# Row maxima of the attention scores: one pair of 64-row matmuls and one reduction of two PSUM banks, in place of two 128-row matmuls and two reductions

## The chip, the cores and the metric

The kernel runs on one core of one Trainium2 chip. The metric is the device time of a run in microseconds, lower is better. The kernel before took 4128.93 us, the median of three runs (4126.80 to 4134.72).

## The reference

```
x: (16, 32, 32, 512) float32, 16 batches of 1024 tokens with 512 channels
qkv = x @ w_qkv + b_qkv                       # 8 heads, q, k, v of 64 channels each
attn = softmax(q @ k.T * 64 ** -0.5)          # 1024 x 1024 for each head
res = (attn @ v) @ w_out + b_out + x
```

All inputs and the output are float32. For every batch and head the softmax runs over 1024 keys for each of 1024 queries.

## The kernel before, in words

Every value that goes through TensorE in the projections and scores is split into a high part (f32r) and a low part, so that a product is several matmuls. Vectors q and k of a head lie in 64 partitions. `k_lo_hi` holds the low part of k in partitions 0 to 63 and the high part in 64 to 127; `q_hi_hi` holds the high part of q twice, in 0 to 63 and again in 64 to 127 (the second copy is made by a DMA, L355). Both are double buffered by head.

A batch is 8 heads of 2 halves of the queries; head and half together are a **unit**, 16 in a batch. A unit has 512 queries (4 tiles of 128) and goes over 1024 keys in 4 **steps** of 256 keys, 64 steps in a batch. The work is laid out by hand in **slots**, one for each step, with some ahead of the first step (slots -5 to -1) and some behind the last. Each engine walks through the same slots, and within one engine everything runs in the written order. In slot s TensorE does, in this order (L605 on):

- the "early" row-maximum tiles of a unit that starts later (L543),
- parts of the q and k projection of a coming head, 12 matmuls for each half of the tokens (L514; in slots with s mod 8 = 0 after the scores),
- the scores of step s + 1 (L572, L574: two key tiles, each two matmuls of 128 rows and 512 columns, each into one of three score banks),
- the "late" row-maximum tiles,
- in one slot of four, a transpose of the unit's row maxima (L552),
- the product of the probabilities and v for step s - 1 (L595, L598: 16 short f16 matmuls).

ScalarE computes the exponentials twice for each score bank (L696 in f32, L697 in f16). GpSimd (L411) or VectorE (L826) takes their difference, the low part of the probabilities, for which L598 waits.

The row maximum is the shift of the softmax. Before the scores of a unit start, it is taken from separate scores: for each of the 4 query tiles and each half of the keys one matmul (L545) with 128 rows in the contraction, `q_hi_hi` against `k_lo_hi`, so q_hi k_lo + q_hi k_hi. This makes 8 tiles for a unit, tile n being query tile n // 2 and key half n % 2. They use PSUM banks 4 and 5 in turn. VectorE reduces each tile of 128 x 512 to one column (L804), and after the eighth joins the pairs (L810). The transpose (L552) turns the 4 columns of maxima into 4 rows, and VectorE writes them, negated, into rows of `q_shift` (L817), by which the second matmul of each score (L574) subtracts the maximum.

A bank is claimed by `claim_max` (L475): tile number n in the order of all maxima and shifts of the batch waits until VectorE has finished number n - 2. So one tile can be written while the one before it is reduced. The order is in `MAX_TILES` (L60): for unit u the slots 4u - 5 to 4u - 2 hold the tiles (0, 1) early and 2 late; (3, 4) early; (5, 6) early and 7 late; none. The transpose of unit u stands in slot 4u - 2. Units 0 and 1 have orders of their own (L61).

## Time and profile before

| what | value |
|---|---|
| median of three runs | 4128.93 us |
| span of the profiled execution | 4126.3 us |
| TensorE busy | 95% |
| ScalarE busy | 75% |
| VectorE busy | 65% |
| GpSimd busy | 52% |
| mean granted TensorE clock | 0.997 |

The profile shows one execution. The busy time of an engine is the time in which at least one of its instructions was under way. Matmuls overlap, and their ends are modelled, so what one costs is read as the distance from its start to the start of the next one. A wait is listed as idle time ahead of an instruction, with the instruction that released it.

### The profile page before, as it was taken

Reading aid. Unit: us, or ns where it says so; the run is one execution under the profiler, and the core shown is the slowest. Engines: PE = TensorE matmul, PEld = TensorE weight load, DVE = VectorE, ACT = ScalarE, POOL = GpSimd, SP = SyncE. Lnnn points to the kernel's source line nnn. Section 1 sums busy time; section 2 is a strip of 40 time slices with the busy share of each in tenths; the row PEclk is TensorE's granted clock in tenths of the full one; section 3 lists DMA queues with packets and bytes.
Section 4 is the critical chain, followed back from the end, with each engine's and each line's share of the span. In section 5 each row is a group of like instructions: output and inputs, shape, how many; then the busy total and the mean of one; then the engine's idle time right before and its main releaser. Section 6 shows DMA issues by size and latency. Waiting matters only on the chain.

```text
span 4126.3 us, 94307 instructions
## 1 busy us (share of the span) xinstructions
PE 3939.8 (95%) x29964; PEld 3064.1 (74%) x29964; DVE 2694.0 (65%) x4395; ACT 3076.7 (75%) x5269; POOL 2135.8 (52%) x1144
## 2 busy tenths in 40 slices
PE   6999999999999999999999999999999999999999
PEld 5777777777777777777777777777777777777777
DVE  5757757576575765757657576675766757667576
ACT  4967949689495895958859588595886959769597
POOL 1645626456263563636636366363663626536265
PEclk9999999999999999999999999999999999999999
DMA  3011020110202102020021201212011121120201
GB/s 97 22 53 43 18 77 23 58 37 17 78 22 66 29 19 75 22 73 22 24 70 23 72 22 29 65 24 73 22 37 58 24 71 24 37 58 22 63 22 42
DMA packets 100814, 179.08 MB, mean 43 GB/s; under 512 B 16192, under 2 KB 16192, under 8 KB 100288
## 3 DMA queue, kind: packets, MB, share of 16 engines
q1 hardware_dynamic: 100288, 172.29, 14.7%
q8 instruction: 302, 4.95, 0.5%
q14 instruction: 224, 1.84, 0.1%
HBM read 71.57 MB, written 33.55 MB: 25 GB/s over the span
## 4 chain that ended last, share of the span: by engine, by line
PE 74%; issue 8%; ACT 8%; DVE 4%; POOL 4%; ACTq 0%; DMA 0%; DVEq 0%; SPq 0%; POOLq 0%
PE psum L514 33%; PE psum L545 10%; PE psum L572 8%; PE psum L595 8%; PE psum L574 7%; ACT p_hi L697 4%; PE psum L598 4%; POOL p_lo L411 4%; ACT p_full L696 3%; PE psum L528 2%; DVE max_parts L804 1%; DVE q_shift L783 1%; ACT k_lo_hi L667 1%; DVE xT_lo L767 1%; DVE q_shift L817 1%
## 5 line engine op out<-in xcount | busy, mean ns | idle before, releaser
L411 POOL TENSOR_TENSOR p_lo<-p_full,p_hi 128x1024 f16<-128x1024 f32 x752 | 1610.5, 2144 | 1452.7 <-ACT p_hi L697 1452.7
L804 DVE TENSOR_REDUCE max_parts<-psum 128x1 f32<-128x512 f32 x2048 | 1341.4, 686 | 534.0 <-PE psum L545 522.6
L696 ACT ACTIVATE p_full<-psum,prob_bias 128x512 f32<-128x512 f32 x2048 | 1434.9, 701 | 123.2 <-PE psum L574 90.6
L697 ACT ACTIVATE p_hi<-psum,prob_bias 128x512 f16<-128x512 f32 x2048 | 1435.6, 701 | 0.0
L595 PEld LDWEIGHTS psum<-v_parts,p_hi 128*128 128x128 f16 x8192 | 714.8, 97 | 284.4 <-issue 133.2
L595 PE MATMUL psum<-v_parts,p_hi 128*128 128x129 f16 x8192 | 854.4, 221 | 35.3 <-POOL p_lo L411 20.3
L572 PE MATMUL psum<-q_hi_hi,k_lo_hi 128*128 128x512 f32 x2048 | 846.2, 413 | 43.6 <-ACT p_hi L697 38.9
L598 PE MATMUL psum<-v_parts,p_lo 128*128 128x65 f16 x8192 | 819.8, 192 | 0.0
L574 PE MATMUL psum<-q_shift,k_shift 128*128 128x512 f32 x2048 | 804.7, 393 | 0.0
L545 PE MATMUL psum<-k_lo_hi,q_hi_hi 128*128 128x512 f32 x2048 | 757.1, 429 | 19.7 <-DVE q_shift L817 11.9
L598 PEld LDWEIGHTS psum<-v_parts,p_lo 128*128 128x128 f16 x8192 | 723.6, 98 | 2.4
L418 POOL TENSOR_TENSOR o_heads<-o_sum,inv_sum 128x256 f32<-128x256 f32 x256 | 364.6, 1424 | 371.7 <-DVE o_sum L835 371.7
L572 PEld LDWEIGHTS psum<-q_hi_hi,k_lo_hi 128*128 128x128 f32 x2048 | 384.3, 188 | 206.6 <-ACT p_hi L697 145.8
L545 PEld LDWEIGHTS psum<-k_lo_hi,q_hi_hi 128*128 128x128 f32 x2048 | 361.7, 188 | 99.7 <-DVE q_shift L817 23.5
L574 PEld LDWEIGHTS psum<-q_shift,k_shift 128*128 128x128 f32 x2048 | 385.5, 188 | 62.6
L514 PE MATMUL psum<-xT_hi,wqkv_hi 128*128 128x512 f32 x1024 | 413.0, 403 | 0.0
L514 PE MATMUL psum<-xT_hi,wqkv_lo 128*128 128x512 f32 x1024 | 409.3, 400 | 0.0
L514 PE MATMUL psum<-xT_lo,wqkv_hi 128*128 128x512 f32 x1024 | 402.7, 393 | 0.0
L655 ACT CAST xT_hi<-psum 128x512 fp32r<-128x512 f32 x256 | 141.9, 601 | 327.3 <-PE psum L528 326.9
L826 DVE TENSOR_TENSOR p_lo<-p_full,p_hi 128x1024 f16<-128x1024 f32 x272 | 331.4, 1218 | 38.1 <-ACT p_hi L697 38.1
L672 ACT CAST v_parts<-psum 128x512 f16<-128x512 f32 x128 | 75.2, 587 | 358.6 <-PE psum L514 358.6
L817 DVE TENSOR_TENSOR q_shift<-psum,minus_block 4x512 fp32r<-4x512 f32 x256 | 173.6, 678 | 156.8 <-PE psum L552 153.6
(61 smaller groups left out, 4308.2 us busy)
## 6 DMA issues: line engine op xcount, KB each, us to landing
x_in<-in_x SPq DMA_DIRECT2D x128, 256.0 KB, 4.0
k_shift<-k_lo_hi SPq DMA_DIRECT2D x256, 128.0 KB, 2.2
q_hi_hi<-q_hi_hi SPq DMA_DIRECT2D x256, 128.0 KB, 2.3
y_tile<-in_x SPq DMA_DIRECT2D x128, 256.0 KB, 2.7
result<-y_tile SPq DMA_DIRECT2D x128, 256.0 KB, 2.3
o_heads<-in_L_conv_w_qkv SPq DMA_DIRECT2D x12, 256.0 KB, 4.1
o_heads<-in_L_conv_w_out SPq DMA_DIRECT2D x4, 256.0 KB, 4.3
out_bias<-in_L_conv_b_out SPq DMA_DIRECT2D x1, 256.0 KB, 6.2
```

The source lines that it names most:

```text
L411: nc.gpsimd.tensor_tensor(p_lo[:, s % P_SLOTS, :, :], p_full[:, s % 2, :, :], p_hi[:, s % P_SLOTS, :, :], ALU.subtract).then_inc(p_lo_read ...
L418: nc.gpsimd.tensor_tensor(o_heads[:, half * Q_TILES:(half + 1) * Q_TILES, h * DIM:(h + 1) * DIM], o_sum[:, :, :], inv_sum[:, :].rearrange( ...
L514: matmul = nc.tensor.matmul(fill_bank(w), a, b, start=n == 0, stop=n == TERMS - 1)
L545: nc.tensor.matmul(dst, q_hi_hi[:, h % 2, q0:q0 + P], k_lo_hi[:, h % 2, k_half * HALF:(k_half + 1) * HALF], start=True, stop=True).then_in ...
L572: nc.tensor.matmul(score_bank(tile), k_lo_hi[:, h % 2, keys], q_hi_hi[:, h % 2, cols], start=True, stop=False)
L574: nc.tensor.matmul(score_bank(tile), k_shift[:, h % 2, keys], q_shift[:, h % 2, cols], start=False, stop=True).then_inc(scores_ready, 1)
L595: nc.tensor.matmul(pv[:, bank, col:col + PV_W], p_hi[:, s % P_SLOTS, n, qs], v_parts[:, kt, h, 0:PV_W], start=kt == 0 and qt % 2 == 0, sto ...
L598: last = nc.tensor.matmul(pv[:, bank, col + DIM:col + PV_W], p_lo[:, s % P_SLOTS, n, qs], v_parts[:, kt, h, DIM:PV_W], start=False, stop=k ...
L696: nc.scalar.activation(p_full[:, s % 2, n, :], score_bank(tile), ACT.Exp, scale=SCALE, bias=prob_bias[:, :])
L697: nc.scalar.activation(p_hi[:, s % P_SLOTS, n, :], score_bank(tile), ACT.Exp, scale=SCALE, bias=prob_bias[:, :]).then_inc(exp_done, 1)
L804: nc.vector.reduce_max(max_parts[:, u % 2, q_tile, k_half:k_half + 1], max_bank(w), AX.X).then_inc(max_tile_done, 1)
L826: nc.vector.tensor_tensor(p_lo[:, s % P_SLOTS, :, :], p_full[:, s % 2, :, :], p_hi[:, s % P_SLOTS, :, :], ALU.subtract).then_inc(p_lo_read ...
```

## The change

The 8 tiles of a unit become 4, one for each query tile. A tile is now two matmuls with 64 rows each. The first has partitions 0 to 63: q_hi against `k_upper`, a new copy of the high part of k for keys 0 to 511, written to bank 4. The second has partitions 64 to 127: the second copy of q_hi against the high part of k for keys 512 to 1023 as it lies in `k_lo_hi`, written to bank 5. The term q_hi k_lo is no longer in the maximum. Only the second matmul signals. VectorE reduces both banks at once, 128 x 1024 to one column of `row_max`; the partial maxima, the joining reduction (L810) and its semaphore are gone. The tiles of a unit stand in these slots: 0 early and 1 late; 2 early; 3 early; none (units 0 and 1: one early tile in each slot). `claim_max` now waits until VectorE has finished number n - 1, since both banks belong to each tile. The copy `k_upper` is made by one more DMA for each head, between the two DMAs of the first half of the tokens, and the maxima wait for it. The diff, without its blank lines:

```diff
@@ -57,9 +37,11 @@
-MAX_TILES = (((0, 1), (2,)), ((3, 4), ()), ((5, 6), (7,)), ((), ()))
-MAX_TILES_OF_UNIT = {0: (((0, 1), ()), ((2, 3), ()), ((4, 5), ()), ((6, 7), ())),
-                     1: (((0, 1), ()), ((2, 3), ()), ((4, 5), (6,)), ((7,), ()))}
+MAX_TILES = (((0,), (1,)), ((2,), ()), ((3,), ()), ((), ()))
+MAX_TILES_OF_UNIT = {0: (((0,), ()), ((1,), ()), ((2,), ()), ((3,), ())),
+                     1: (((0,), ()), ((1,), ()), ((2,), ()), ((3,), ()))}
 def max_tiles_of_slot(s, late=False):
@@ -68,7 +50,7 @@
     if not 0 <= unit < UNITS:
         return []
     tiles = MAX_TILES_OF_UNIT.get(unit, MAX_TILES)
-    return [("row_max", unit, n // 2, n % 2) for n in tiles[slot][late]]
+    return [("row_max", unit, n) for n in tiles[slot][late]]
 def shift_unit_of_slot(s):
@@ -212,8 +194,6 @@
 def attention_block(nc: bass.Bass, x, w_qkv, b_qkv, w_out, b_out, out):
     f32, f32r, f16 = mybir.dt.float32, mybir.dt.float32r, mybir.dt.float16
     ALU, ACT, AX = mybir.AluOpType, mybir.ActivationFunctionType, mybir.AxisListType
-    assert MAXES % 2 == 0
     x_tok = x.rearrange("b h w c -> b (h w) c")
     out_tok = out.rearrange("b h w c -> b (h w) c")
@@ -235,6 +215,7 @@
         o_heads = sb("o_heads", [P, TOKEN_TILES, CH], f32)
         v_parts = sb("v_parts", [P, TOKEN_TILES, HEADS, V_WIDTH], f16)
         k_lo_hi = sb("k_lo_hi", [P, 2, TOKENS], f32r)
+        k_upper = sb("k_upper", [DIM, 2, HALF], f32r)
         k_shift = sb("k_shift", [P, 2, TOKENS], f32r)
         q_hi_hi = sb("q_hi_hi", [P, 2, TOKENS], f32r)
         q_shift = sb("q_shift", [P, 2, TOKENS], f32r)
@@ -247,7 +228,6 @@
         v_bias = sb("v_bias", [P, CH_TILES], f32)
         out_bias = sb("out_bias", [P, CH], f32)
         minus_block = sb("minus_block", [Q_TILES, Q_TILES, P], f32)
-        max_parts = sb("max_parts", [P, 2, Q_TILES, 2], f32)
         row_max = sb("row_max", [P, 2, Q_TILES], f32)
         o_lo = sb("o_lo", [P, Q_TILES, DIM], f32)
         o_sum = sb("o_sum", [P, Q_TILES, DIM], f32)
@@ -263,8 +243,7 @@
         psum = ctx.enter_context(nc.psum_tensor("psum", [P, 8, HALF], f32))
         pv = psum[:, 6:8, :]
-        def max_bank(w):
-            return psum[:, 4 + MAX_AT[w] % 2, :]
+        max_banks = psum[:, 4:6, :]
         def fill_bank(w):
             return psum[:, FILL_BANK[w], :]
@@ -294,6 +273,7 @@
         hi_done = sem("hi_done")
         max_tile_ready = sem("max_tile_ready")
         max_tile_done = sem("max_tile_done")
+        k_upper_ready = sem("k_upper_ready")
         k_shift_ready = [sem(f"k_shift_ready{k}") for k in range(HALVES)]
         q_hi_hi_ready = [sem(f"q_hi_hi_ready{k}") for k in range(HALVES)]
         scores_ready = sem("scores_ready")
@@ -301,7 +281,6 @@
         p_lo_ready = [sem(f"p_lo_ready{k}") for k in range(2)]
         DVE, POOL = False, True
         pv_done = sem("pv_done")
-        max_ready = sem("max_ready")
         o_lo_ready = sem("o_lo_ready")
         o_free = sem("o_free")
         o_ready = sem("o_ready")
@@ -352,6 +331,9 @@
                         sp.wait_ge(hi_done, signals(i, HIS, HI_AT["qk", h, half] + 1))
                         sp.dma_start(k_shift[DIM:P, h % 2, cols].bitcast(f32),
                                      k_lo_hi[DIM:P, h % 2, cols].bitcast(f32)).then_inc(k_shift_ready[half], 16)
+                        if half == 0:
+                            sp.dma_start(k_upper[:, h % 2, :].bitcast(f32),
+                                         k_lo_hi[DIM:P, h % 2, cols].bitcast(f32)).then_inc(k_upper_ready, 16)
                         sp.dma_start(q_hi_hi[DIM:P, h % 2, cols].bitcast(f32),
                                      q_hi_hi[0:DIM, h % 2, cols].bitcast(f32)).then_inc(q_hi_hi_ready[half], 16)
@@ -475,12 +457,11 @@
                 def claim_max(w):
                     n = MAX_AT[w]
-                    if n < 2:
+                    if n == 0:
                         pe.wait_ge(fill_done, signals_led(i, FILLS, 0))
                     else:
-                        pe.wait_ge(max_tile_done, signals_led(i, MAXES, n - 1))
-                    return max_bank(w)
+                        pe.wait_ge(max_tile_done, signals_led(i, MAXES, n))
                 def three_terms(a_hi, a_lo, b_hi, b_lo):
@@ -535,21 +516,23 @@
                         projection(w, first, last)
                 def row_max_tile(w):
-                    _, u, q_tile, k_half = w
+                    _, u, q_tile = w
                     h, half = divmod(u, HALVES)
-                    dst = claim_max(w)
+                    claim_max(w)
                     pe.wait_ge(fill_done, signals_led(i, FILLS, FILL_AT["qk", h, 1] + 1))
                     pe.wait_ge(q_hi_hi_ready[half], signals(i, HEADS * 16, (h + 1) * 16))
+                    pe.wait_ge(k_upper_ready, signals(i, HEADS * 16, (h + 1) * 16))
                     q0 = half * HALF + q_tile * P
-                    nc.tensor.matmul(dst, q_hi_hi[:, h % 2, q0:q0 + P],
-                                     k_lo_hi[:, h % 2, k_half * HALF:(k_half + 1) * HALF],
+                    nc.tensor.matmul(max_banks[:, 0, :], q_hi_hi[0:DIM, h % 2, q0:q0 + P],
+                                     k_upper[:, h % 2, :], start=True, stop=True)
+                    nc.tensor.matmul(max_banks[:, 1, :], q_hi_hi[DIM:P, h % 2, q0:q0 + P],
+                                     k_lo_hi[DIM:P, h % 2, HALF:2 * HALF],
                                      start=True, stop=True).then_inc(max_tile_ready, 1)
                 def shift_tile(u):
-                    dst = claim_max(("shift", u))
-                    pe.wait_ge(max_ready, signals_led(i, UNITS, u + 1))
-                    nc.tensor.transpose(dst[0:Q_TILES, 0:P], row_max[:, u % 2, :],
+                    claim_max(("shift", u))
+                    nc.tensor.transpose(max_banks[0:Q_TILES, 0, 0:P], row_max[:, u % 2, :],
                                         identity[:, :]).then_inc(max_tile_ready, 1)
                 def step_scores(s):
@@ -757,7 +740,7 @@
             dve.wait_ge(bias_product, 1)
             nc.vector.tensor_tensor(out_bias[:, :], psum[:, 5, :], out_bias[:, :], ALU.add).then_inc(bias_ready, 1)
             dve.wait_ge(consts_ready, 4)
-            for led in (fill_done, max_tile_done, p_lo_ready[DVE], o_free, max_ready):
+            for led in (fill_done, max_tile_done, p_lo_ready[DVE], o_free):
                 dve.sem_inc(led)
             with dve.Fori(0, BATCH) as i:
                 def transposed_lo(w):
@@ -795,20 +778,11 @@
                     {"x_transpose": transposed_lo, "o_transpose": transposed_lo, "v": v_lo, "qk": qk_lo,
                      "project": project_add}[w[0]](w)
-                def row_max_part(w):
-                    _, u, q_tile, k_half = w
+                def row_max_tile(w):
+                    _, u, q_tile = w
                     dve.wait_ge(max_tile_ready, signals(i, MAXES, MAX_AT[w] + 1))
-                    if (q_tile, k_half) == (0, 0):
-                        dve.wait_ge(max_ready, signals_led(i, UNITS, max(u - 1, 0)))
-                    nc.vector.reduce_max(max_parts[:, u % 2, q_tile, k_half:k_half + 1], max_bank(w),
-                                         AX.X).then_inc(max_tile_done, 1)
-                def join_max(u):
-                    dve.wait_ge(max_tile_done, signals_led(i, MAXES, MAX_AT["row_max", u, Q_TILES - 1, 1] + 1))
-                    nc.vector.tensor_reduce(row_max[:, u % 2, :], max_parts[:, u % 2, :, :], AX.X,
-                                            ALU.max).then_inc(max_ready, 1)
+                    nc.vector.reduce_max(row_max[:, u % 2, q_tile:q_tile + 1],
+                                         max_banks.rearrange("p b k -> p (b k)"), AX.X).then_inc(max_tile_done, 1)
                 def shift_rows(u):
                     h, half = divmod(u, HALVES)
@@ -816,7 +790,7 @@
                     dve.wait_ge(max_tile_ready, signals(i, MAXES, MAX_AT[w] + 1))
                     nc.vector.tensor_tensor(
                         q_shift[0:Q_TILES, h % 2, half * HALF:(half + 1) * HALF].rearrange("r (t q) -> r t q", q=P),
-                        max_bank(w)[0:Q_TILES, 0:P].rearrange("r (o q) -> r o q", o=1).broadcast_to([Q_TILES, Q_TILES, P]),
+                        max_banks[0:Q_TILES, 0, 0:P].rearrange("r (o q) -> r o q", o=1).broadcast_to([Q_TILES, Q_TILES, P]),
                         minus_block[:, :, :], ALU.mult).then_inc(max_tile_done, 1)
                 def step_lo(s):
@@ -846,9 +820,7 @@
                         for w in consumed_in_slot(s):
                             take(w)
                     for w in max_tiles_of_slot(s):
-                        row_max_part(w)
-                        if w[2:] == (Q_TILES - 1, 1):
-                            join_max(w[1])
+                        row_max_tile(w)
                     if s < 0:
                         for w in consumed_in_slot(s):
                             take(w)
@@ -857,9 +829,7 @@
                     if 0 <= s < STEPS and not on_pool(s):
                         step_lo(s)
                     for w in max_tiles_of_slot(s, late=True):
-                        row_max_part(w)
-                        if w[2:] == (Q_TILES - 1, 1):
-                            join_max(w[1])
+                        row_max_tile(w)
                     if 0 <= s < STEPS:
                         for w in consumed_in_slot(s):
                             take(w)
```

## Rows read from the trace of the kernel before

**Rows 1.** The page, part 1: busy us of each engine, share, instructions.

```profile
PE 3939.8 (95%) x29964; PEld 3064.1 (74%) x29964; DVE 2694.0 (65%) x4395; ACT 3076.7 (75%) x5269; POOL 2135.8 (52%) x1144
```

**Rows 2.** One head in the middle of a batch: windows, all instructions and then L545 alone.

```profile
core 0: us, PE busy (x) PEld busy (x) DVE busy (x) ACT busy (x) POOL busy (x), PEclk, DMA share, GB/s
900.20:924.60 24.40, 24.04 (x207) 18.57 (x204) 17.77 (x31) 22.35 (x39) 15.95 (x9) 1.00 0.10 23
...
900.20:924.60 24.40, 5.93 (x16) 2.81 (x16) 1.00 0.10 23
```

**Rows 3.** Timeline of an even unit: start us, us, engine, line, operation, count.

```profile
899.79 0.68 DVE L817 TENSOR_TENSOR q_shift<-psum,minus_block 4x512 fp32r<-4x512 f32 x1
...
900.27 0.75 PE L545 MATMUL psum<-k_lo_hi,q_hi_hi 128*128 128x512 f32 x2
...
902.02 0.40 PE L545 MATMUL psum<-k_lo_hi,q_hi_hi 128*128 128x512 f32 x1
...
902.45 0.69 DVE L804 TENSOR_REDUCE max_parts<-psum 128x1 f32<-128x512 f32 x1 [0.29 <-PE psum L545]
...
903.07 0.70 PE L545 MATMUL psum<-k_lo_hi,q_hi_hi 128*128 128x512 f32 x2
...
903.58 1.29 DVE L804 TENSOR_REDUCE max_parts<-psum 128x1 f32<-128x512 f32 x2 [0.44 <-PE psum L545]
903.61 0.40 PE L514 MATMUL psum<-xT_lo,wqkv_hi 128*128 128x512 f32 x1
...
905.00 0.40 PE L574 MATMUL psum<-q_shift,k_shift 128*128 128x512 f32 x1
...
905.94 0.71 PE L545 MATMUL psum<-k_lo_hi,q_hi_hi 128*128 128x512 f32 x2
...
906.49 0.39 PE L514 MATMUL psum<-xT_lo,wqkv_hi 128*128 128x512 f32 x1
```

**Rows 4.** Timeline of the odd unit behind it, same columns.

```profile
911.49 0.68 DVE L817 TENSOR_TENSOR q_shift<-psum,minus_block 4x512 fp32r<-4x512 f32 x1 [1.42 <-PE psum L552]
...
911.98 0.74 PE L545 MATMUL psum<-k_lo_hi,q_hi_hi 128*128 128x512 f32 x2
...
912.58 2.04 DVE L804 TENSOR_REDUCE max_parts<-psum 128x1 f32<-128x512 f32 x3 [0.41 <-PE psum L545]
...
913.50 0.40 PE L545 MATMUL psum<-k_lo_hi,q_hi_hi 128*128 128x512 f32 x1
913.52 0.68 ACT L667 ACTIVATE k_lo_hi<-psum,qk_bias 64x512 fp32r<-64x512 f32 x1
...
915.01 0.39 PE L572 MATMUL psum<-q_hi_hi,k_lo_hi 128*128 128x512 f32 x1
915.24 0.40 PE L574 MATMUL psum<-q_shift,k_shift 128*128 128x512 f32 x1
...
915.55 0.50 PE L572 MATMUL psum<-q_hi_hi,k_lo_hi 128*128 128x512 f32 x1
915.88 0.40 PE L574 MATMUL psum<-q_shift,k_shift 128*128 128x512 f32 x1
```

**Rows 5.** The page, part 5, groups by line: busy us, mean ns, idle before, releasers.

```profile
L804 DVE TENSOR_REDUCE max_parts<-psum 128x1 f32<-128x512 f32 x2048 | 1341.4, 686 | 534.0 <-PE psum L545 522.6
...
L545 PE MATMUL psum<-k_lo_hi,q_hi_hi 128*128 128x512 f32 x2048 | 757.1, 429 | 19.7 <-DVE q_shift L817 11.9
...
L826 DVE TENSOR_TENSOR p_lo<-p_full,p_hi 128x1024 f16<-128x1024 f32 x272 | 331.4, 1218 | 38.1 <-ACT p_hi L697 38.1
```

**Rows 6.** Timeline where TensorE waited for the shift, as rows 3.

```profile
924.51 0.68 DVE L817 TENSOR_TENSOR q_shift<-psum,minus_block 4x512 fp32r<-4x512 f32 x1
...
925.24 0.19 PEld L545 LDWEIGHTS psum<-k_lo_hi,q_hi_hi 128*128 128x128 f32 x1 [0.42 <-DVE q_shift L817]
```

**Rows 7.** Timeline of TensorE in the projections ahead of a batch's first step.

```profile
830.13 0.62 PE L545 MATMUL psum<-k_lo_hi,q_hi_hi 128*128 128x512 f32 x2
830.59 0.39 PE L514 MATMUL psum<-wqkv_hi,xT_hi 128*128 128x512 f32 x1
```

**Rows 8.** The page, part 6, DMA issues: out<-in, queue, count, KB each, us to landing.

```profile
k_shift<-k_lo_hi SPq DMA_DIRECT2D x256, 128.0 KB, 2.2
```

## The prediction

> **What bounds the kernel now.** I read the busy times of the page first, then one head from the middle of a batch as a window, then the timeline around the row-maximum tiles. TensorE is busy for 3939.8 of 4126.3 us [rows 1], and in the head of 24.40 us for 24.04 us, at full granted clock (1.00, the 2.4 GHz level); ScalarE follows with 22.35 us [rows 2]. So over the seven heads of a batch that look like this one, time that TensorE loses by waiting is lost to the whole, and time that it is spared is gained until ScalarE's 22.35 us are reached. Of the 24.04 us, the intervals of L545 take 5.93 us [rows 2]; they are what the change works on. Inside a slot TensorE executes in written order, so a row-maximum tile that waits holds up the probabilities-times-v product, the next fills and the next scores behind it, and through the scores ScalarE.
>
> **What the change does on TensorE.** A late tile costs 0.23 us now: behind the matmul at 905.00 the next work comes one such pitch later, and 0.23 is also the distance 915.01 to 915.24 [rows 3, 4]. Two tiles right behind the short f16 matmuls take 903.61 - 903.07 = 0.54 us or 906.49 - 905.94 = 0.55 us [rows 3], so 0.31 for the first and 0.23 for the second: 0.08 to 0.10 us of weight load lies bare (915.55 to 915.88 is 0.33 against 0.23 with the load covered [rows 4]). Call it 0.09.
>
> A pair of 64-row matmuls is not in the trace. From below it is one matmul of today, 0.23 us; from above two of them one behind the other, 0.46 us; to both comes the bare load where the engine has just waited or done short matmuls. I take the second matmul as running beside the first but starting one bare load later: 0.23 + 0.09 = 0.32 us, and 0.41 us behind a wait or short matmuls. That value is near the lower end, and in places behind a wait or short matmuls both loads must be done in any case before both matmuls can stream.
>
> **What the change does on VectorE.** Now a tile of 128 x 512 takes 0.686 us [rows 5], two in a row 1.29 us from start to end [rows 3]. For 128 x 1024 in one instruction the nearest row is L826 with that shape and 1.218 us [rows 5]; two tiles in a row give 1.29 as the other end. I take 1.22. VectorE is busy for 17.77 of 24.40 us [rows 2], so the small saving there and the vanished joining reduction are worth nothing by themselves.
>
> **The new wait.** The important part is `claim_max`. With both banks used by each tile, tile n + 1 can't be started before the reduction of tile n has ended. The cycle from one tile to the next comes out as follows. From a matmul L545 with a bare load to the start of VectorE: 912.58 - 911.98 = 0.60 us [rows 4] (without one 902.45 - 902.02 = 0.43 [rows 3]). The second half-matmul comes 0.09 later: 0.69. Reduction 1.22. Back to TensorE: the shift ends at 924.51 + 0.68 = 925.19 and the load waiting for it starts at 925.24, so 0.05 [rows 6]. Sum 1.96 us.
>
> Between tile 0 (early) and tile 1 (late, same slot) TensorE has one projection matmul at most and four score matmuls, 5 x 0.23 = 1.15 us; with the tile's own 0.41 it would be back after 1.56, so 0.4 us of waiting. Between tile 1 and tile 2 (early in the next slot) it has only the 16 short matmuls, from 905.00 + 0.23 = 905.23 to 905.94 = 0.71 us [rows 3]; with 0.41 that is 1.12, so 0.84 us of waiting. Between tiles 2 and 3 lie a slot's scores, its short matmuls and fills; there I cost the wait at nothing. Tile 0 also has to wait for the shift of the unit before, which only the second tile had to do until now.
>
> Even unit [rows 3]: the shift ends at 899.79 + 0.68 = 900.47, tile 0 starts at 900.52, tile 1 at 902.48, tile 2 at 904.44, and the work behind it at 904.85. Today that work (L514) starts at 903.61: 1.24 us later. In the next slot but one the change gives back: 0.55 for two early tiles and 0.23 for the late one become 0.41, so 0.37. Net +0.87 us.
>
> Odd unit [rows 4]: shift end 912.17, tiles at 912.22, 914.18 and 916.14, next work at 916.55 against 915.01 today: +1.54. Behind it TensorE waits for ScalarE now (915.24 to 915.55 and 915.55 to 915.88 where 0.23 would do): 0.18 of the delay vanishes there. Giving back the same 0.37: +0.99 us.
>
> Units 2 to 15 of each of 16 batches go this way, 224 units. At the mean of 0.93 us they cost 208 us. I apply this to the last two units of a batch as well, though these have no projections beside them; ScalarE is near its limit there, but a delay of about 2 us within two slots is beyond what its queue of three score banks holds.
>
> Units 0 and 1 are in stretches dense with projections, with a tile per slot and no such wait. There a pair costs 830.59 - 830.13 = 0.46 us today [rows 7] and 0.32 after: 0.14 x 4 for unit 0 and 3 times for unit 1, whose tile 0 waits for its shift, so about 1 us of a batch and -16 us in all.
>
> Edits at nothing: the added DMA for each head. The high part of k for the first half is written from 913.52 to 914.20 [rows 4], such a copy lands 2.2 us behind its issue [rows 8], and the next head's tile 0 is the first reader, whose second matmul stands at 925.24 [rows 6]: some 8 us of cover; without that cover it would cost up to 2.2 us a head, 282 us. It is issued by SP ahead of the first half's copy of q_hi, which has the same cover.
>
> Sum: 4126.3 + 208 - 16 = 4318 us for the profiled span; the median of the runs is 2.6 us above the span today. **4320 us.**
>
> **The rivals.**
>
> *Both at once, 4240 us.* The halves start together and the load of the second is covered. Then a cycle is 1.87, and each of the tiles is 0.09 shorter: 4 x 0.09 = 0.36 us for a unit, 81 us in all. For it: TensorE already runs loads beside matmuls. Against it: the bare load behind short matmuls and waits is visible, and here there are two. The Trainium skill, TensorE: Matmul & The Clock Gate, section Part 3: Packing small matmuls — row/col tiling, says that matmuls in different row groups start about 4 ns apart; no row here shows it, and by it this would be the outcome.
>
> *Not side by side, 4440 us.* The second half starts when the first has streamed, a full pitch of 0.23 later in place of 0.09. That is 0.14 for each tile: 4 x 0.14 = 0.56 us for a unit, 256 units make 143 less some cover by waits, about 120. For it: no row shows two matmuls at once. This is the case in which the change doesn't do what it says.
>
> *A price for changing between 128 and 64 rows, 4520 us.* Each pair is surrounded by 128-row matmuls. If the array must empty at each change, a matmul's way through it is bare: 0.39 duration less 0.23 pitch, 0.16 us [rows 3], with a bare load of 0.09 behind it. Where TensorE waits anyway this is hidden; open are leaving tile 2 (0.25), entering (0.16) and leaving (0.25) tile 3: 0.66 for each of 224 units, 148 us, and about 0.4 for each of 8 tiles in units 0 and 1, 51 us. In all +199. For it: nothing in the trace, as all matmuls have 128 rows. The Trainium skill, TensorEngine Tiling (Array Packing), section Tiling Modes, under Key Properties, states that changing the tiling mode drains TensorE; it speaks against the change, and by it this case would be the outcome.
>
> *The wait is covered, 4000 us.* If TensorE's new waits fell into time in which it waits for ScalarE or GpSimd anyway, only the shorter stream would count: 0.59 for the first two tiles (900.27 to 900.86) against 0.41, 0.23 against 0.32, 0.54 against 0.41, 0.78 against 0.41, so -0.59 us a unit, 132 for 224 units, and the 16. That gives 3980, with what ScalarE's waits keep back about 4000. It decides from the point where TensorE has 1.55 us of other work between tiles 1 and 2; I see 0.71, and a head with only 0.36 us in which TensorE isn't busy [rows 2].
>
> **How the numbers follow.** My forecast 0.42, both at once 0.13, not side by side 0.13, the price of the change of rows 0.20, covered 0.09, and 0.03 that waits and gains cancel. The range of 4210 to 4520 leaves out the last two and the upper part of the dear case, together under 0.2. A measurement of this kernel can tell 0.2%, about 8 us. Faster 0.09, the same 0.03, slower 0.88.
>
> **What would show it.** The waits on TensorE: L545's successor should show idle time released by VectorE's maximum, near 0.4 and 0.84 us for each of 224 units, some 280 us in total, where L545 has 19.7 us of idle time ahead of it now [rows 5]. Starts of the pair 0.09 apart (0.23: not side by side; 0.00: both at once). The matmul behind tile 3 in its slot should follow 0.32 behind the pair's start plus at most the bare load; over 0.5 means that the change of rows costs. The reduction should last 1.22 us. TensorE's busy time should fall while the head grows from 24.4 to about 26.3 us. I am wrong if the head period stays at 24.4 or falls, that is, if the distance from tile 1 to tile 2 is near 1.1 us instead of 1.96.

## The result, and the profile after

The changed kernel takes 4407.86 us (median of 4 runs, 4406.26 to 4408.48) against 4129.45 us for the kernel before (median of 4): 1.0668 times the time before, 95% interval 1.0655 to 1.0682. It is slower by 278 us. The prediction said 4320 us, range 4210 to 4520. All times compared here are of fast executions; one of the four of experiment 4 took 13800 us at a granted clock of 0.555, the other three 4240.7 to 4243.0.

The page of the kernel after, parts 1 and 5 (it answers to [rows 1, 5]):

```profile
span 4406.7 us, 91090 instructions
...
PE 4013.4 (91%) x29964; PEld 2891.5 (66%) x29964; DVE 2581.2 (59%) x3115; ACT 3083.5 (70%) x5269; POOL 2128.6 (48%) x1144
...
L784 DVE TENSOR_REDUCE row_max<-psum 128x1 f32<-128x1024 f32 x1024 | 1253.8, 1224 | 760.9 <-PE psum L529 756.4
...
L527 PE MATMUL psum<-k_upper,q_hi_hi 64*128 64x512 f32 x1024 | 504.9, 493 | 214.8 <-DVE row_max L784 143.4
```

TensorE's busy time did not fall, it rose from 3939.8 us [rows 1] to 4013.4, though the same 29964 matmuls include 1024 pairs that run side by side. And TensorE now idles ahead of L527 for 214.8 us where L545 had 19.7 [rows 5]. These are two separate losses: a wait, and time in which the array is held. VectorE's reduction of 128 x 1024 takes 1.224 us, as taken from L826 [rows 5].

A head from the middle of a batch, as a window (it answers to [rows 2]):

```profile
960.15:987.05 26.90, 24.59 (x202) 17.28 (x203) 17.22 (x20) 22.43 (x39) 15.91 (x9) 1.00 0.11 26
```

The head grew from 24.4 to 26.9 us, at the same granted clock of 1.00. The first loss, the wait, is seen in the list of waits of the same run (engine, line waited, releaser: us in total, times, longest):

```profile
PEld psum L527 <- DVE row_max L784: 282.9, 480, 0.7
PE psum L527 <- DVE row_max L784: 143.4, 368, 0.5
PEld psum L527 <- issue: 84.0, 176, 0.9
PE psum L527 <- DVE q_shift L791: 55.1, 128, 1.0
```

PEld is the weight load, PE the matmul behind it; their waits overlap and are not to be added. 480 is two tiles in each of the 224 units that were forecast (448), and tiles 1 and 2 of unit 1 with 16 each.

The timeline of an even unit after the change (it answers to [rows 3]; start us, us, engine, line, operation, count, idle before and its releaser):

```profile
960.22 0.47 PE L527 MATMUL psum<-k_upper,q_hi_hi 64*128 64x512 f32 x1 [0.35 <-DVE q_shift L791]
960.22 0.18 PEld L529 LDWEIGHTS psum<-k_lo_hi,q_hi_hi 64*128 64x128 f32 x1
960.23 0.49 PE L529 MATMUL psum<-k_lo_hi,q_hi_hi 64*128 64x512 f32 x1
960.65 0.19 PEld L495 LDWEIGHTS psum<-xT_hi,wqkv_hi 128*128 128x128 f32 x1 [0.24 <-issue]
960.65 0.50 PE L495 MATMUL psum<-xT_hi,wqkv_hi 128*128 128x512 f32 x1
960.75 0.19 PEld L555 LDWEIGHTS psum<-q_hi_hi,k_lo_hi 128*128 128x128 f32 x1
960.75 1.23 DVE L784 TENSOR_REDUCE row_max<-psum 128x1 f32<-128x1024 f32 x1 [0.86 <-PE psum L529]
960.99 0.40 PE L555 MATMUL psum<-q_hi_hi,k_lo_hi 128*128 128x512 f32 x1
...
962.03 0.18 PEld L527 LDWEIGHTS psum<-k_upper,q_hi_hi 64*128 64x128 f32 x1 [0.39 <-DVE row_max L784]
...
963.85 0.50 PE L527 MATMUL psum<-k_upper,q_hi_hi 64*128 64x512 f32 x1 [0.52 <-DVE row_max L784]
```

From tile to tile it is 962.03 - 960.22 = 1.81 and 963.85 - 962.03 = 1.82 us, and 0.53 + 1.23 + 0.05 makes that up: pair to reduction (960.22 to 960.75), reduction, and back. The two matmuls of a pair start 0.00 to 0.01 us apart, so they do run side by side. The second loss is behind them: the load of the next 128-row weights doesn't begin beside the pair, it begins at 960.65, 0.43 us after the pair's start, and the matmul it belongs to takes 0.34 us until the next start (960.65 to 960.99) where 0.23 is usual. So 512 columns, streamed once, hold TensorE for 0.43 + 0.11 = 0.54 us. The pair also starts late when nothing blocks it: 0.12 us behind the last short matmul instead of 0.03, so 0.09 ahead of it (experiment 9 shows both lines).

### The profile page after: what moved, and what is told of

It is laid out like the page before. It is cut to its first block, busy times and chain, and to the rows that moved or that the text cites. A ratio compares the mean times of both kernels' runs of the same rounds, so it can differ in the third digit from the quotient of the medians.

```text
span 4406.7 us, 91090 instructions
## 1 busy us (share of the span) xinstructions
PE 4013.4 (91%) x29964; PEld 2891.5 (66%) x29964; DVE 2581.2 (59%) x3115; ACT 3083.5 (70%) x5269; POOL 2128.6 (48%) x1144
## 4 chain that ended last, share of the span: by engine, by line
PE 70%; DVE 16%; issue 6%; ACT 6%; POOL 2%; ACTq 0%; DMA 0%; SPq 0%; DVEq 0%; POOLq 0%
PE psum L495 34%; DVE row_max L784 11%; PE psum L527 11%; PE psum L555 8%; PE psum L557 7%; PE psum L578 4%; DVE q_shift L791 4%; ACT p_hi L680 2%; PE psum L581 2%; PE psum L509 2%; ACT p_full L679 2%; POOL p_lo L393 2%; ACT k_lo_hi L650 1%; PE psum L535 1%; DVE q_shift L766 1%
## 5 line engine op out<-in xcount | busy, mean ns | idle before, releaser
L784 DVE TENSOR_REDUCE row_max<-psum 128x1 f32<-128x1024 f32 x1024 | 1253.8, 1224 | 760.9 <-PE psum L529 756.4
L555 PE MATMUL psum<-q_hi_hi,k_lo_hi 128*128 128x512 f32 x2048 | 873.5, 427 | 59.7 <-ACT p_hi L680 56.7
L527 PE MATMUL psum<-k_upper,q_hi_hi 64*128 64x512 f32 x1024 | 504.9, 493 | 214.8 <-DVE row_max L784 143.4
L529 PE MATMUL psum<-k_lo_hi,q_hi_hi 64*128 64x512 f32 x1024 | 508.6, 497 | 0.0
L527 PEld LDWEIGHTS psum<-k_upper,q_hi_hi 64*128 64x128 f32 x1024 | 187.1, 183 | 433.3 <-DVE row_max L784 282.9
L495 PE MATMUL psum<-xT_hi,wqkv_hi 128*128 128x512 f32 x1024 | 437.8, 427 | 0.0
L495 PE MATMUL psum<-xT_lo,wqkv_hi 128*128 128x512 f32 x1024 | 423.6, 414 | 0.0
L791 DVE TENSOR_TENSOR q_shift<-psum,minus_block 4x512 fp32r<-4x512 f32 x256 | 173.6, 678 | 298.0 <-PE psum L535 298.0
```

The costliest lines, as they stand in the source:

```text
L495: matmul = nc.tensor.matmul(fill_bank(w), a, b, start=n == 0, stop=n == TERMS - 1)
L527: nc.tensor.matmul(max_banks[:, 0, :], q_hi_hi[0:DIM, h % 2, q0:q0 + P], k_upper[:, h % 2, :], start=True, stop=True)
L529: nc.tensor.matmul(max_banks[:, 1, :], q_hi_hi[DIM:P, h % 2, q0:q0 + P], k_lo_hi[DIM:P, h % 2, HALF:2 * HALF], start=True, stop=True).then ...
L555: nc.tensor.matmul(score_bank(tile), k_lo_hi[:, h % 2, keys], q_hi_hi[:, h % 2, cols], start=True, stop=False)
L784: nc.vector.reduce_max(row_max[:, u % 2, q_tile:q_tile + 1], max_banks.rearrange("p b k -> p (b k)"), AX.X).then_inc(max_tile_done, 1)
```

## The experiments

All were timed in three groups, each group on one chip together with the kernel before. The medians of the kernel before were 4134.42 us for the first four, 4131.66 for the next four, 4133.68 for the last three. The changed kernel has only its own 4408 us, so a difference to it is good to about 5 us. In the diffs, `...` stands for what is left out.

Small differences need one more reading of the traces. Every unit ends its maxima with one `q_shift<-psum,minus_block` on VectorE (L817 before, L791 after), called the shift. The distance from the last shift of a batch to the first of the next, here called the turn, is one of two in every run: in the profiled execution of the kernel before 7 of the 15 turns took 76.0 to 76.2 us and 8 took 77.6 to 77.9, in the changed kernel 11 took 76.7 to 77.0 and 4 took 78.4. A long and a short one of the changed kernel, 347.71 - 269.32 = 78.39 and 620.28 - 543.54 = 76.74:

```profile
269.32 0.68 DVE L791 TENSOR_TENSOR q_shift<-psum,minus_block 4x512 fp32r<-4x512 f32 x1 [1.03 <-PE psum L535]
347.71 0.67 DVE L791 TENSOR_TENSOR q_shift<-psum,minus_block 4x512 fp32r<-4x512 f32 x1
...
543.54 0.68 DVE L791 TENSOR_TENSOR q_shift<-psum,minus_block 4x512 fp32r<-4x512 f32 x1 [1.02 <-PE psum L535]
620.28 0.67 DVE L791 TENSOR_TENSOR q_shift<-psum,minus_block 4x512 fp32r<-4x512 f32 x1
```

Long and short ones come in no fixed order, and the cause is open. So two runs can differ by some 20 us without any edit being the cause. Between the first and last shift of a batch there is no such jump. Summed over the batches of each profiled execution, in us more than the kernel before:

| run | inside the batches | the 15 turns | whole span |
|---|---|---|---|
| changed kernel | +275 | +5 | +280 |
| experiment 4 | +105 | +7 | +112 |
| experiment 5 | +244 | +11 | +257 |
| experiment 6 | +74 | -3 | +72 |
| experiment 8 | +34 | -13 | +20 |
| experiment 10 | +17 | +16 | +33 |
| experiment 11 | +264 | +15 | +279 |

**1. 64 rows in the kernel before.** The matmul of L545:

```diff
-nc.tensor.matmul(dst, q_hi_hi[:, h % 2, q0:q0 + P], k_lo_hi[:, h % 2, ...], ...)
+nc.tensor.matmul(dst, q_hi_hi[DIM:P, h % 2, q0:q0 + P], k_lo_hi[DIM:P, h % 2, ...], ...)
```

> The kernel before, with one edit: each of its 8 row-maximum tiles of a unit multiplies partitions 64 to 127 only (64 rows, the term q_hi k_lo is left out of the maximum). Banks in turn, order and waits as before, nothing side by side. Theory 1 (a change between 128 and 64 rows costs TensorE time, about 0.1 us ahead of the matmul and 0.3 us behind it, as the trace of the changed kernel shows around its pairs): five groups of such tiles in a unit, 0.3 to 0.4 us each, some 1250 groups, so 4450 to 4600 us. Rival (the price lies in the pair or in the waits for VectorE alone, 64 rows cost nothing): 4129 us within 0.3%.

Measured 4404.97 us, 1.0654 (1.0636 to 1.0672), 270 us more. The lower end of theory 1 was missed by 45 us, the rival is out: fewer rows alone, one matmul behind the other, cost about as much as the whole change did. TensorE is busy for 97% of the span. The page and the timeline of this run:

```profile
PE 4280.6 (97%) x29964; PEld 3035.8 (69%) x29964; DVE 2699.1 (61%) x4395; ACT 3106.4 (71%) x5269; POOL 2129.5 (48%) x1144
...
939.39 0.73 PE L545 MATMUL psum<-k_lo_hi,q_hi_hi 64*128 64x512 f32 x2
940.05 0.50 PE L514 MATMUL psum<-xT_lo,wqkv_hi 128*128 128x512 f32 x1
940.38 0.40 PE L514 MATMUL psum<-xT_hi,wqkv_lo 128*128 128x512 f32 x1
...
942.08 0.49 PE L545 MATMUL psum<-k_lo_hi,q_hi_hi 64*128 64x512 f32 x1
942.51 0.23 PE L595 MATMUL psum<-v_parts,p_hi 128*128 128x129 f16 x1
```

Two tiles take 940.05 - 939.39 = 0.66 us in place of 0.54 [rows 3], and the L514 behind them 0.33 in place of 0.23. Part of the load is bare behind a 64-row matmul here, for a second 64-row matmul in the same partitions too: the median of its distance from the first is 0.34 us. A lone 64-row matmul holds TensorE for 942.51 - 942.08 = 0.43 us, as long as a pair side by side.

**2. 128 rows in the changed kernel.** The copy `k_upper` and the wait for it are left out too.

```diff
-matmul(max_banks[:, 0, :], q_hi_hi[0:DIM, ...], k_upper[:, h % 2, :])
-matmul(max_banks[:, 1, :], q_hi_hi[DIM:P, ...], k_lo_hi[DIM:P, h % 2, HALF:2 * HALF])
+matmul(max_banks[:, 0, :], q_hi_hi[:, ...], k_lo_hi[:, h % 2, 0:HALF])
+matmul(max_banks[:, 1, :], q_hi_hi[:, ...], k_lo_hi[:, h % 2, HALF:2 * HALF])
```

> The changed kernel with 128-row matmuls in its tiles (two, one behind the other, as before the change, and no copy k_upper): no change of rows, nothing side by side, but the single-buffered banks, one reduction of 128 x 1024, and the new order. Theory 1 (the wait for VectorE is the larger part): a cycle from tile to tile of 0.83 + 1.22 + 0.05 = 2.1 us, two of them a unit, so about +1.2 us for each of 224 units: 4370 to 4450 us. Rival (the change of rows is nearly all of it): 4129 to 4200 us.

Measured 4492.0 us, 1.0866 (1.0848 to 1.0884), 358 us more, above the range of theory 1; the rival is out. Its waits:

```profile
PEld psum L523 <- DVE row_max L780: 344.5, 464, 0.8
```

With 128-row matmuls, the single pair of banks and the order of its tiles cost more than the whole change. Against it, the pair of 64 rows in the changed kernel is a gain of 84 us.

**3. The reduction cut short.**

```diff
-max_banks.rearrange("p b k -> p (b k)")
+max_banks[:, 1, 0:P]
```

> The changed kernel with its reduction cut to 128 columns of the second bank (the maximum is taken over 128 keys, the rest is left out). Matmul pairs, order and semaphores unchanged; the reduction takes about 0.3 us in place of 1.22, so no tile waits for the one before it. Theory 1: the wait's share goes, the price of the change of rows stays (0.1 to 0.2 us for each of 1024 pairs): 4230 to 4300 us. Rival (waits are hidden by others behind them): above 4350 us. Rival (the change of rows costs nothing): below 4100 us.

Measured 4196.31 us, 1.0153 (1.0136 to 1.0170): below theory 1's range, and neither of the rivals. Its reduction and what is left of TensorE's idle time ahead of the pairs:

```profile
L784 DVE TENSOR_REDUCE row_max<-psum 128x1 f32<-128x128 f32 x1024 | 298.5, 291 | 1227.9 <-PE psum L529 1223.5
...
L527 PE MATMUL psum<-k_upper,q_hi_hi 64*128 64x512 f32 x1024 | 504.8, 493 | 71.3 <-DVE q_shift L791 55.1
```

With a reduction of 0.29 us no wait on the maximum is left in that line, and 212 of the 278 us are gone. What a short reduction also does is to free VectorE for its other work, so 212 is taken as an upper bound for the wait.

**4. The tiles spread.**

```diff
-MAX_TILES = (((0,), (1,)), ((2,), ()), ((3,), ()), ((), ()))
+MAX_TILES = (((0,), ()), ((1,), ()), ((2,), (3,)), ((), ()))
```

> The changed kernel with its four tiles spread over the slots: 0 early; 1 early; 2 early and 3 late; none, in place of 0 early and 1 late; 2 early; 3 early. Everything else unchanged. Theory 1: both waits of 0.4 and 0.8 us in a unit go, since scores and products lie between the tiles, except a short one ahead of tile 3 in the last heads: 4240 to 4320 us. Rival (the order doesn't matter, as TensorE loses its time to the change of rows): 4380 to 4410 us.

Measured 4242.9 us, 1.0264 (1.0243 to 1.0284). Theory 1 holds: 165 us are won by order alone, with the full reduction.

```profile
PEld psum L527 <- DVE row_max L784: 36.0, 64, 0.6
PE psum L527 <- DVE q_shift L791: 107.0, 128, 1.0
```

The waits on the maximum fell from 480 to 64; tile 3 of the last two units of a batch makes 32 of these, tiles 1 and 2 of unit 1 the other 32. The wait of tile 0 for the shift grew in return, from 55.1 to 107.0 us.

**5. The wait for the banks last.** In `row_max_tile` of TensorE:

```diff
-claim_max(w)
 pe.wait_ge(fill_done, ...)
 pe.wait_ge(q_hi_hi_ready[half], ...)
 pe.wait_ge(k_upper_ready, ...)
+claim_max(w)
```

> The changed kernel with one edit on TensorE: in a row-maximum tile the wait for the banks stands behind the waits for the fill and the copies, no longer ahead of them. In the trace of the changed kernel the first tile of an even unit starts 0.29 us after the shift that it waits for, in an odd unit 0.05 us; in the even ones TensorE's queue still works through the other waits after the shift's. Theory 1: about 0.24 us for each of 8 even units of 16 batches, 31 us at most: 4375 to 4385 us. Rival (the delay has another cause, or is hidden): 4408 us within 0.2%.

Measured 4385.93 us, 1.0618 (1.0600 to 1.0636), 22 us under the changed kernel. Theory 1 holds, a little outside its range in the total, and inside the batches with 275 - 244 = 31 us. The changed kernel at the first tile of an even unit:

```profile
986.07 0.68 DVE L791 TENSOR_TENSOR q_shift<-psum,minus_block 4x512 fp32r<-4x512 f32 x1 [0.68 <-PE psum L535]
987.04 0.18 PEld L527 LDWEIGHTS psum<-k_upper,q_hi_hi 64*128 64x128 f32 x1 [0.47 <-issue]
```

and the same place in experiment 5:

```profile
953.93 0.68 DVE L790 TENSOR_TENSOR q_shift<-psum,minus_block 4x512 fp32r<-4x512 f32 x1 [0.67 <-PE psum L534]
954.66 0.18 PEld L526 LDWEIGHTS psum<-k_upper,q_hi_hi 64*128 64x128 f32 x1 [0.23 <-DVE q_shift L790]
```

The load starts 987.04 - 986.75 = 0.29 us after the shift's end in the first, 954.66 - 954.61 = 0.05 in the second. In the first the three later waits stood behind the one that blocked and were worked off only after it. In the median it is 0.30 against 0.05, in each of the 7 even units of a batch that wait for a shift (the expectation counted 8), 112 places. In odd units it was 0.05 before the edit already; why they don't show it is open.

**6. Both edits, 4 and 5.**

> The two edits together: tiles spread over the slots as in the run before it of that name, and the wait for the banks last. Theory 1: both gains add up, 4243 - 30 = 4210 to 4220 us, still above the kernel before by the price of the change of rows. Rival (the price of the change of rows is small and was mostly waiting): 4140 us or less.

Measured 4198.48 us, 1.0160 (1.0143 to 1.0177). It is below the forecast range. Inside the batches the second edit wins 105 - 74 = 31 us, as it did in experiment 5: there the gains add up; the rest of the 44 us against experiment 4 lies mostly in the turns. It is the best version with the full maximum and the pair, and still 67 us behind the kernel before.

**7. Not side by side.** Both matmuls of a tile use `q_hi_hi[DIM:P]` and `k_lo_hi[DIM:P]`; the copy `k_upper` and the wait for it are left out.

> The changed kernel with both 64-row matmuls of a tile on partitions 64 to 127 (k_lo_hi for both halves of the keys, no copy k_upper), so that they can't run side by side. Banks, order, waits and reduction unchanged. Theory 1: the second starts 0.34 us behind the first, as two such matmuls did in the kernel with 64 rows and banks in turn; 0.33 us for each of 1024 tiles, a tile-to-tile cycle of 2.15 in place of 1.82: 4650 to 4740 us. Rival (the pair's side-by-side running is worth nothing, since its load or the waits hide it): 4408 to 4450 us.

Measured 4617.35 us, 1.1180 (1.1162 to 1.1199): 209 us above the changed kernel, somewhat below theory 1's range; the rival is out.

```profile
990.54 0.50 PE L523 MATMUL psum<-k_lo_hi,q_hi_hi 64*128 64x512 f32 x1 [0.17 <-DVE row_max L780]
990.88 0.39 PE L525 MATMUL psum<-k_lo_hi,q_hi_hi 64*128 64x512 f32 x1
991.20 0.23 PE L574 MATMUL psum<-v_parts,p_hi 128*128 128x129 f16 x1
```

The second starts 0.34 us after the first as said, but the next matmul comes only 0.32 behind it, not 0.43: the tile takes 0.66 us in place of 0.43, so side by side is worth 0.23 us a tile, not 0.33. Here 1024 x 0.23 = 236 us are near the 209 measured.

**8. The spread order in the kernel before.**

```diff
-MAX_TILES = (((0, 1), (2,)), ((3, 4), ()), ((5, 6), (7,)), ((), ()))
+MAX_TILES = (((0, 1), ()), ((2, 3), ()), ((4, 5), (6, 7)), ((), ()))
```

> The kernel before (128 rows, banks in turn) with its 8 tiles of a unit in another order: (0, 1) early; (2, 3) early; (4, 5) early and (6, 7) late; none. It is the control for the spread order, which in the changed kernel gained 165 us. Theory 1 (that gain came from the waits on the single pair of banks, which this kernel doesn't have): 4120 to 4145 us. Rival (the order itself is the better one, by balance between the slots): 4000 to 4100 us.

Measured 4148.55 us, 1.0040 (1.0026 to 1.0055), slightly above theory 1's range: the order gains nothing by itself, it loses 17 us (34 inside the batches). So the 165 us of experiment 4 are waits.

**9. Pairs in the middle of the f16 matmuls.** On the code of 6, tiles 0, 1 and 3 of units 2 to 13 are issued from within `step_pv`, VectorE's order follows:

```diff
 for n in range(KEYS_PER_STEP):
     kt = key_tile(s, n)
+    if n == 1:
+        for w in between:
+            row_max_tile(w)
```

> The run with spread tiles and the wait for the banks last, with its tiles of units 2 to 13 moved once more: 0, 1 and 3 in the middle of the 16 short f16 matmuls of their slot, 2 between the fills and the scores. Units 0, 1, 14 and 15 as in that run. Theory 1 (a pair costs 0.09 us on entering and 0.43 us of its own in any place, but the bare load of the next 128-row f32r matmul, 0.11 us, only where such a one follows): a pair among f16 matmuls costs 0.52 us in place of 0.63, three of them in 12 units of 16 batches 0.33 x 192 = 63 us less, and tile 0 needs no wait for the shift any more, up to 0.3 us x 192: 4080 to 4140 us against 4198 of that run. Rival (the price is the same at every place, or VectorE now comes too late for the unit's output): 4190 us or more.

Measured 4349.53 us, 1.0524 (1.0509 to 1.0538), 151 us worse than 6: the forecast failed, the rival holds for the total. At the place itself the price is as said:

```profile
926.38 0.19 PE L587 MATMUL psum<-v_parts,p_lo 128*128 128x65 f16 x1
926.50 0.50 PE L530 MATMUL psum<-k_upper,q_hi_hi 64*128 64x512 f32 x1
926.50 0.50 PE L532 MATMUL psum<-k_lo_hi,q_hi_hi 64*128 64x512 f32 x1
926.94 0.23 PE L584 MATMUL psum<-v_parts,p_hi 128*128 128x129 f16 x1
```

0.12 in place of 0.03 ahead of the pair, 0.44 for it, and nothing more. But the transpose of the maxima now waits for tile 3's reduction in 144 units:

```profile
PEld psum L538 <- DVE row_max L792: 106.2, 144, 1.2
PE psum L538 <- DVE row_max L792: 43.7, 144, 0.8
```

That explains part of the 151 us. The rest may lie in VectorE's new order in the slots with fills; it was not taken apart.

**10. Experiment 6 with the short reduction of 3.**

> The run with spread tiles and the wait for the banks last, with its reduction cut to 128 columns of one bank (the maximum is taken over 128 keys). What is left above the kernel before is then the change of rows alone. Theory 1 (the waits are gone already, only those of the last two units of a batch and of the transpose go): 4165 to 4190 us. Rival (a good part of the remaining 67 us is still waiting): 4130 us or less.

Measured 4162.46 us, 1.0075 (1.0059 to 1.0090), just under theory 1's range; the rival is out. With the waits for a long reduction gone and the order spread, the kernel is still 29 us behind the one before. But it isn't shown that these 29 us are the price of the rows alone, as was expected. In the profiled executions 16 of 33 us lie in the turns. And TensorE still waits for the shift ahead of tile 0 in all 240 places:

```profile
PEld psum L526 <- DVE q_shift L790: 72.7, 240, 1.4
...
944.75 0.19 PE L580 MATMUL psum<-v_parts,p_lo 128*128 128x65 f16 x1
945.01 0.50 PE L526 MATMUL psum<-k_upper,q_hi_hi 64*128 64x512 f32 x1
```

945.01 - 944.75 = 0.26 us in place of the 0.12 of a pair that nothing blocks, some 30 us over the run (an estimate, 0.14 x 224); and the same order cost the kernel before 17 us. So whether a better arrangement of the waits could have made the pairs pay is open. The price of the pair on TensorE is known at its place, and how much of it reaches the total isn't shown.

**11. No copy.** No DMA to `k_upper` and no wait for it; the first matmul reads `k_lo_hi[0:DIM]`.

> The changed kernel without its added DMA and the wait for it: the first half of the tile takes partitions 0 to 63 of k_lo_hi (the low part of k) as moving operand, so the maximum of keys 0 to 511 is of the wrong product. Theory 1 (the copy is hidden): 4400 to 4410 us. Rival (the copy delays the other copies behind it on SP, or its wait costs a turn of TensorE's queue in even units, 0.09 us each): 4390 us or less.

Measured 4407.42 us, 1.0661 (1.0645 to 1.0678), in theory 1's range. The trace says something else on the wait:

```profile
959.62 0.68 DVE L787 TENSOR_TENSOR q_shift<-psum,minus_block 4x512 fp32r<-4x512 f32 x1 [0.67 <-PE psum L531]
960.52 0.18 PEld L523 LDWEIGHTS psum<-k_lo_hi,q_hi_hi 64*128 64x128 f32 x1 [0.39 <-issue]
```

In even units the load now starts 960.52 - 960.30 = 0.22 us after the shift, in place of 0.30: the one wait less saves 0.08 us, as the rival had it, and the batches are 12 us shorter inside. The total hides it, because 12 of the 15 turns were long ones in this execution, 4 in that of the changed kernel. That the DMA itself cost anything is shown nowhere.

## Why the prediction was right, point by point

The corners, the left column with the tiles in the order of the kernel before, the right one in that of the kernel after:

| row maximum by | banks in turn | both banks for each tile |
|---|---|---|
| 128 rows | 4129 to 4134 (before) | 4492 (2) |
| 64 rows, one after another | 4405 (1) | 4617 (7) |
| 64 rows, side by side | not possible in two banks | 4408 (after) |

**The new wait: right in mechanism and place.** It decides between tiles 0, 1 and 2, in 224 units; experiments 2, 3, 4 and 8 show it from four sides. It is worth 165 us by order alone and about 212 at most. The cycle was forecast at 1.96 us and is 1.82: the term too long was the 0.69 us from the start of a pair to the reduction, 0.53 in the trace. The halves start together, which takes 0.09 off; the other 0.07 lies in the 0.60 taken from [rows 4], where 0.43 [rows 3] and a bare load of 0.09 would have given 0.52. The reduction (1.22) and the way back (0.05) were as taken.

**The pair on TensorE: the term that was mis-sized.** I took 0.32, or 0.41 behind a wait or short matmuls. It is 0.43 in either place, with 0.11 us more on the next f32r matmul and about 0.09 on the matmul ahead of it. Tile 3 of a unit, forecast to give back 0.37 us, gives 0.78 - (0.09 + 0.43 + 0.11) = 0.15. I had made "both at once" and "a price for changing between 128 and 64 rows" rivals of each other and of the forecast, with 0.13 and 0.20. Both are true together: starts 0.00 apart, and a bare exit. The price of 0.66 us a unit in the dear case was too high: by the same count it is 0.54 - 0.41 = 0.13 on leaving tile 2 and 0.63 - 0.41 = 0.22 around tile 3, 0.35 in all.

**Units 0 and 1: wrong in sign at the place.** In the kernel after, in the projections ahead of a batch:

```profile
880.06 0.50 PE L527 MATMUL psum<-k_upper,q_hi_hi 64*128 64x512 f32 x1
...
880.49 0.50 PE L495 MATMUL psum<-wqkv_hi,xT_hi 128*128 128x512 f32 x1
880.83 0.39 PE L495 MATMUL psum<-wqkv_lo,xT_hi 128*128 128x512 f32 x1
```

0.43 + 0.11, with 0.09 ahead, is 0.63 where it was 0.46 [rows 7]: +0.17 for each of 8 tiles of 16 batches, +22 us in place of -16 (an estimate). From shift to shift, the trace has +7 us for unit 1 over the run, and +5 for the turns, in which unit 0 lies.

**The wait for the shift: too small.** I put tile 0 0.05 us behind it; in even units it is 0.29 to 0.30, for the reason of experiment 5: 31 us inside the batches, 22 in the total.

**The sum again with these sizes.** Even unit from the shift's end: 0.29 + 3.64 + 0.43 + 0.11 = 4.47, against 903.61 - 900.47 = 3.14 before [rows 3], +1.33, and -0.15. Odd: 0.05 + 3.64 + 0.54 = 4.23 against 915.01 - 912.17 = 2.84 [rows 4], +1.39, -0.15, and -0.18 for ScalarE. The mean is 1.12 us; 224 units make 251, with the 22 above 273 of the 278 us measured. That it comes so near is partly luck: from shift to shift the 224 units give 1.20 us each, 268 us, and units 0 and 1 and the turns 12. The head of the two windows grew by 26.90 - 24.40 = 2.50 us where the sum has 1.18 + 1.06 = 2.24. What makes the other 0.26 wasn't taken apart. The forecast had 0.93 and -16. It was low by 88 us because of the pair's exit and the queue's other waits. The shorter cycle worked the other way, by 2 x 0.14 us a unit or 63 us: with the right cycle and the other terms as they were, the forecast would have been about 4257 us and the miss larger.

**The rivals.** "Covered" (4000 us) fell: it needed 1.55 us of work between tiles 1 and 2. "Not side by side" fell by the starts, and experiment 7 prices it at +209 us, where I had about +120: each tile's 0.23 us weighs almost in full. The DMA was hidden, as said; its wait on TensorE was not, at 0.08 us in even units (experiment 11). TensorE's busy time was forecast to fall and rose; that row alone points at the exit's price.

The Trainium skill, TensorE: Matmul & The Clock Gate, section Part 3: Packing small matmuls — row/col tiling, has the halves about 4 ns apart; the trace agrees with 0.00 to 0.01 us. The Trainium skill, TensorEngine Tiling (Array Packing), section Tiling Modes, says that a change of tiling mode drains TensorE; the trace is in line with it: the next 128-row load begins 0.43 us after the pair's start, where between 128-row matmuls it runs beside the matmul ahead.

## What to carry to other kernels

Before packing matmuls into halves of the array, add up what surrounds each packed group: here one pair of 64-row matmuls cost 0.63 us between long 128-row matmuls, against 0.46 for the two it replaced, and 0.52 where short f16 matmuls followed. Whether several packed groups in a row share one entry and one exit, no run here tried. A tile that takes both banks of a double buffer turns every reader's time into a distance between writers; work out that distance (write, reduction, way back) and place the tiles at least that far apart. Where several waits stand ahead of an instruction, put the one that blocks last. Before you read a difference of 20 us off two totals, look whether it lies where the edit is.

## What was not expected of the hardware

- Two 64-row matmuls in the same partitions, one behind the other, start 0.34 us apart, against 0.23 us for 128 rows in a stream: the load of the second isn't fully covered by the first (experiments 1 and 7). Behind a wait two 128-row matmuls start 0.34 us apart too (experiment 2: medians of tiles 1 and 2).
- After a wait that blocks, TensorE's queue needed 0.24 us for three further waits that had long been met (0.29 against 0.05 us), 31 us over the batches (experiment 5); with one of them gone it needed 0.08 less (experiment 11).
- The exit from 64 rows depends on what ran: 0.43 us from the start of a pair side by side, or of a lone 64-row matmul (experiment 1), to the next matmul, but 0.32 from the start of the second of two in the same partitions (experiment 7).
- The turn between two batches takes one of two durations, 1.6 us apart, in every run; the cause is open.
